# Cross-attention in a perceiver block: the low parts of 64 context channels by another route, and three scalings on ScalarE

## The reference, cut to what matters

```python
xn = layernorm(ctx, ln_x_g, ln_x_b)               # 8 x 1601 x 192
ln = layernorm(latents, ln_l_g, ln_l_b)           # 8 x 64 x 256
q  = ln @ Wq.T
kv = concat([xn @ Wkv.T, ln @ Wlkv.T], axis=1)    # 1665 keys and values
k, v = kv[..., :256], kv[..., 256:]               # 4 heads of 64
attn = (rmsnorm(q, qn_g) * 64**-0.5) @ rmsnorm(k, kn_g).T      # masked
out  = softmax(attn) @ v                          # then Wo, bias, residual
```

## Time and profile before

| what | value |
|---|---|
| runs | 520.67 us median of 3 (520.42 to 523.8) |
| the profiled execution | 520.81 us, its span 519.0 us |
| granted TensorE clock, mean | 0.964 |
| busy: PE, DVE, ACT, POOL | 83%, 78%, 46%, 48% |
| loop over the 56 groups | from 51.8 us (first `key_sums`) to some 325 us |
| mixer and experts | from some 357 us to the end |

### The profile page before, as it was taken

How to read it: one execution, slowest core, us unless ns; L and a number is a source line. 1 busy time by engine, 2 the same in 40 slices (tenths; PEclk the granted TensorE clock), 3 DMA queues, 4 the chain that set the end, 5 groups by cost and what they waited for, 6 DMA issues and landing times.

```text
span 519.0 us, 6624 instructions
## 1 busy us (share of the span) xinstructions
PE 431.1 (83%) x2042; PEld 334.5 (64%) x2042; DVE 405.3 (78%) x969; ACT 237.8 (46%) x547; POOL 250.3 (48%) x264
## 2 busy tenths in 40 slices
PE   3786557779799889887998988887997877899996
PEld 0364335567677677675786867774474765678885
DVE  5847799999999999999988896625659556887776
ACT  0238645267466564664654744331233125335551
POOL 5451956658558557576484553001431232445550
PEclk9999988889999999999899999899999988889999
DMA  8605842022141041222200000920000000000001
GB/s 248 179 1 148 237 135 56 2 90 53 51 141 50 3 141 50 76 67 58 90 3 1 1 1 15 406 97 0 0 2 0 1 0 0 1 1 1 0 2 41
DMA packets 23976, 31.80 MB, mean 61 GB/s; under 512 B 2955, under 2 KB 19653, under 8 KB 23941
## 3 DMA queue, kind: packets, MB, share of 16 engines
q1 hardware_dynamic: 23940, 31.38, 19.6%
HBM read 30.69 MB, written 0.52 MB: 60 GB/s over the span
## 4 chain that ended last, share of the span: by engine, by line
DVE 34%; PE 30%; POOL 21%; issue 8%; ACT 4%; DMA 2%; SPq 1%; DVEq 0%; POOLq 0%; ACTq 0%
PE bank L573 29%; POOL kr L483 12%; DVE kss L1397 5%; DVE arena L1409 4%; DVE arena L1445 3%; DVE split_b L1388 3%; POOL crs L448 3%; DVE cst L1334 2%; DVE arena L1604 2%; DVE arena L1618 1%; DVE kguard L1400 1%; POOL split_b L472 1%; DVE big L1319 1%; POOL cguard L449 1%; DMA mask_in<-in_p_mask 1%
## 5 line engine op out<-in xcount | busy, mean ns | idle before, releaser
L573 PE MATMUL bank<-keyq,split_b 128*128 128x512 f32 (+2 forms) x724 | 171.0, 384 | 21.2 <-DVE split_b L1678 6.7
L573 PEld LDWEIGHTS bank<-keyq,split_b 128*128 128x128 f32 (+1 forms) x724 | 124.7, 194 | 51.3 <-issue 18.0
L483 POOL TENSOR_TENSOR kr<-kguard,neg_half 128x8 f32<-128x8 f32 (+1 forms) x56 | 94.4, 1686 | 103.5 <-DVE kguard L1400 103.1
L573 PE MATMUL bank<-arena 128*128 128x193 f32 (+4 forms) x528 | 103.4, 340 | 18.5 <-ACT arena L1133 9.0
L573 PEld LDWEIGHTS bank<-arena 128*128 128x128 f32 (+2 forms) x528 | 86.9, 195 | 31.1 <-issue 13.9
L1126 ACT ACTIVATE arena<-bank 128x512 f32<-128x512 f32 (+1 forms) x56 | 31.5, 563 | 59.9 <-PE bank L573 59.4
L573 PE MATMUL bank<-split_b,keyq 128*128 128x512 f32 x204 | 51.7, 405 | 0.1
L1409 DVE TENSOR_TENSOR arena<-bank,kr 128x512 f32<-128x512 f32 (+1 forms) x56 | 36.1, 645 | 19.3 <-POOL kr L483 19.1
L1388 DVE TENSOR_TENSOR split_b<-arena,split_b 32x256 fp32r<-32x256 f32 (+1 forms) x112 | 48.0, 428 | 2.5
L573 PEld LDWEIGHTS bank<-split_b,keyq 128*128 128x128 f32 x204 | 39.1, 197 | 8.0 <-DVE split_b L1669 0.2
L472 POOL TENSOR_TENSOR split_b<-arena,split_b 128x256 fp32r<-128x256 f32 (+1 forms) x56 | 38.2, 682 | 10.1 <-ACT split_b L1109 10.0
(11 more groups left out here) (222 smaller groups left out, 620.5 us busy)
## 6 DMA issues: line engine op xcount, KB each, us to landing
arena<-in_ctx SPq DMA_DIRECT2D x16, 576.0 KB, 4.4
arena<-in_p_ctxT SPq DMA_DIRECT2D x8, 800.5 KB, 6.7
arena<-in_p_ctxT SPq DMA_DIRECT2D x8, 400.2 KB, 7.1
arena<-in_p_experts SPq DMA_DIRECT2D x1, 2688.0 KB, 18.4
arena<-in_p_experts SPq DMA_DIRECT2D x1, 2304.0 KB, 12.2
arena<-in_p_experts SPq DMA_DIRECT2D x1, 1536.0 KB, 6.4
X<-in_x SPq DMA_DIRECT2D x1, 512.0 KB, 3.7
arena<-in_t_Wlkv SPq DMA_DIRECT2D x1, 512.0 KB, 7.0
```

Source lines behind the costliest of these rows:

```text
L483: pool.tensor_tensor(kr[0:r, n % 2, 0:k], kg_[0:r, n % 2, 0:k], neg_half[0:r, 0:4 * k].rearrange("p (t h) -> p t h", h=H), ALU.pow).then_i ...
L573: return nc.tensor.matmul(out_, l, r, start=start, stop=stop, skip_group_check=shared)
```

## The change

1. `split_side` goes from VectorE. POOL subtracts instead, right after `split_rest(n)`: one operation of 64 partitions x 256 into a new tile `side_low` (two buffers). ScalarE then issues two SBUF-to-SBUF DMAs per group, each of 32 partitions x 1 KB, that bring it to partitions 96 to 127 (`move_side`). TensorE's `keys(n)` waits for the transfers.
2. ScalarE's split becomes two functions with a semaphore each. In step g = 5, `split_small(u+2)`, with the wait for `spread_sd`, moves behind `square_keys(u)`.
3. `evac_sum`: VectorE keeps the reduction and the reciprocal, ScalarE scales and copies, two operations of 128 x 193. `evac_latent_out` goes to ScalarE, two of 128 x 128. `max_diagonal`: VectorE keeps the reduction, ScalarE makes the diagonals, two of 128 x 128.
4. `cguard` goes: line 1400 takes the larger of `cve` times 64e-16 and the plain sum of squares, both 64 times what they were, so that the power -0.5 now holds the factor 64**-0.5 too; `qkg` loses that factor, and the copy of the latents' scores gets it.

```diff
@@ gpsimd
-                then(pool.tensor_scalar(cguard[:, k, of], cve[:, k, of], 1e-16, None, ALU.mult))
...
                 pool.tensor_tensor(v[:, 1, 0:k], raw[:, 0], v[:, 0, 0:k].bitcast(F32), ALU.subtract).then_inc(xs_rest, 1)
+                pool.wait_ge(xs_small, n + 1)
+                if n >= 2:
+                    pool.wait_ge(side_in[(n - 2) % 3], 32 * ((n - 2) // 3 + 1))
+                pool.tensor_tensor(side_low[:, n % 2, 0:k], raw[0:SMALL, 1], v[0:SMALL, 2, 0:k].bitcast(F32), ALU.subtract).then_inc(xs_side, 1)
@@ tensor, keys(n)
-                pe.wait_ge(xs_side, n + 1)
+                pe.wait_ge(side_in[n % 3], 32 * (n // 3 + 1))
@@ scalar
                 if g == 0:
                     act.wait_ge(ctxT_in[b % 2], 48 * (b // 2 + 1))
-                    act.wait_ge(sd_in[b % 2], 32 * (b // 2 + 1))
...
-                A(xs[n % 3][:, 0, 0:k], ctxT[b % 2][:, 0, 256 * g:256 * g + k], ACT.Copy)
-                A(xs[n % 3][0:96, 2:4, 0:k], ctxT[b % 2][0:96, 1:2, 256 * g:256 * g + k].broadcast_to([96, 2, k]), ACT.Copy).then_inc(xs_split, 1)
+                A(xs[n % 3][:, 0, 0:k], ctxT[b % 2][:, 0, 256 * g:256 * g + k], ACT.Copy).then_inc(xs_split, 1)
+
+            def split_small(n):
...
+                if g == 0:
+                    act.wait_ge(sd_in[b % 2], 32 * (b // 2 + 1))
+                k = 256 if g < NG - 1 else TAIL
+                A(xs[n % 3][0:96, 2:4, 0:k], ctxT[b % 2][0:96, 1:2, 256 * g:256 * g + k].broadcast_to([96, 2, k]), ACT.Copy).then_inc(xs_small, 1)
+
+            def move_side(n):
...
+                act.wait_ge(xs_side, n + 1)
+                for j in range(2):
+                    act.dma_start(xs[n % 3][96:P, 2 + j, 0:k].bitcast(F32), side_low[32 * j:32 * j + 32, n % 2, 0:k].bitcast(F32)).then_inc(side_in[n % 3], 16)
...
+            def max_diagonal(b):
+                act.wait_ge(col_max, b + 1)
+                for pair in range(NPAIR):
+                    last = A(diag[:, pair, :], ident[:], ACT.Copy, scale=qmax[:, pair:pair + 1])
...
+            def evac_sum(b):
+                act.wait_ge(rl_ready, b + 1)
...
+                for pair in range(NPAIR):
+                    last = A(ysb[:, pair, :], y_bank[:, pair * D:pair * D + ROW], ACT.Copy, scale=rl[:, pair:pair + 1])
...
+            def evac_latent_out(b):
+                act.wait_ge(olat_mm, b + 1)
...
+                    last = A(olat[:, pair, :], misc[:, pair * P:(pair + 1) * P], ACT.Copy, scale=rl[:, pair:pair + 1])
...
@@ scalar, the loop
-            split_high(0)
-            split_high(1)
+            for n in range(2):
+                split_high(n)
+                split_small(n)
+            for n in range(2):
+                move_side(n)
...
                 if u + 2 < groups:
                     split_high(u + 2)
+                    if g != 5:
+                        split_small(u + 2)
...
                 if u < groups:
                     square_keys(u)
+                if g == 5 and u + 2 < groups:
+                    split_small(u + 2)
+                if u + 2 < groups:
+                    move_side(u + 2)
...
+                if g == 1 and 1 <= b <= B:
+                    max_diagonal(b - 1)
...
+                if g == 3 and 2 <= b <= B + 1:
+                    evac_sum(b - 2)
+                    evac_latent_out(b - 2)
@@ vector
-                for j in range(2):
-                    last = V.tensor_tensor(v[96:P, 2 + j, 0:k], side_[32 * j:32 * j + 32], v[32 * j:32 * j + 32, 2 + j, 0:k].bitcast(F32), ALU.subtract)
-                last.then_inc(xs_side, 1)
...
-                V.scalar_tensor_tensor(kg_[0:r, n % 2, 0:k], kss[0:r, n % 2, 0:k], 1.0 / DH,
-                                       cguard[0:r, b % 2, 2 * g:2 * g + k].unsqueeze(2).broadcast_to([r, k, H]), ALU.mult, ALU.max).then_inc(k_ss, 1)
+                V.scalar_tensor_tensor(kg_[0:r, n % 2, 0:k], cve[0:r, b % 2, 2 * g:2 * g + k].unsqueeze(2).broadcast_to([r, k, H]), DH * 1e-16,
+                                       kss[0:r, n % 2, 0:k], ALU.mult, ALU.max).then_inc(k_ss, 1)
...
-                then(V.reciprocal(rl[:], lsum[:]))
                 if b:
-                    dve.wait_ge(yT_mm, b)
-                V.tensor_tensor(ysb[:], y[:, :, 0:ROW], rl[:].unsqueeze(2).broadcast_to([P, NPAIR, ROW]), ALU.mult).then_inc(y_evac, 1)
...
+                    dve.wait_ge(olat_evac, b)
+                V.reciprocal(rl[:], lsum[:]).then_inc(rl_ready, 1)
```

More of the change, by code:

```diff
@@ L177, in build @@
         csd = sb("csd", [P, FULL + 1])
-        cguard = sb("cguard", [P, 2, FULL + 1])
         sdT = sb("sdT", [FULL + 1, P])
+        side_low = sb("side_low", [SMALL, 2, 256], F32R)
         sd_part = sb("sd_part", [FULL + 1, 2, P], F32R)
@@ L1136, in exponentials @@
                     A(lat_tile(b), lat_tile(b), ACT.Exp).then_inc(exp_done, 1)
+            def max_diagonal(b):
+                act.wait_ge(col_max, b + 1)
+                for pair in range(NPAIR):
+                    last = A(diag[:, pair, :], ident[:], ACT.Copy, scale=qmax[:, pair:pair + 1])
+                last.then_inc(max_diag, 1)
+            def evac_sum(b):
+                act.wait_ge(rl_ready, b + 1)
+                if b:
+                    act.wait_ge(yT_mm, b)
+                for pair in range(NPAIR):
+                    last = A(ysb[:, pair, :], y_bank[:, pair * D:pair * D + ROW], ACT.Copy, scale=rl[:, pair:pair + 1])
+                last.then_inc(y_evac, 1)
+            def evac_latent_out(b):
+                act.wait_ge(olat_mm, b + 1)
+                if b:
+                    act.wait_ge(o_mm, b)
+                for pair in range(NPAIR):
+                    last = A(olat[:, pair, :], misc[:, pair * P:(pair + 1) * P], ACT.Copy, scale=rl[:, pair:pair + 1])
+                last.then_inc(olat_evac, 1)
             def evac_max(b):
@@ L1435, in max_diagonal @@
                 dve.wait_ge(maxT_mm, b + 1)
-                then(V.tensor_reduce(qmax[:], misc[:, 0:D].rearrange("p (j k) -> p j k", j=NPAIR), AX.X, ALU.max))
-                V.tensor_tensor(diag[:], ident[:].unsqueeze(1).broadcast_to([P, NPAIR, P]), qmax[:].unsqueeze(2).broadcast_to([P, NPAIR, P]), ALU.mult).then_inc(max_diag, 1)
+                V.tensor_reduce(qmax[:], misc[:, 0:D].rearrange("p (j k) -> p j k", j=NPAIR), AX.X, ALU.max).then_inc(col_max, 1)
             def shift_scores(m):
@@ L1526, in _ @@
                 fold_low_part(j)
-            split_side(0)
-            split_side(1)
             for n in range(NG, LEAD):
@@ L1543, in _ @@
                     evac_sum(b - 2)
-                if g == 4 and 2 <= b <= B + 1:
-                    evac_latent_out(b - 2)
                 if g == 1 and 1 <= b <= B:
@@ L1549, in _ @@
                     shift_scores(u - SHIFT)
-                if u + 2 < groups:
-                    split_side(u + 2)
                 if u + LEAD < groups:
```

22 lines of the change are left out of this document (7 added, 15 removed).

## The result

The changed kernel takes 543.71 us (median of 4, 542.5 to 545.71) against 522.0 before (median of 4): ratio 1.042, 95% interval 1.037 to 1.047. It is slower by 4%, and outside the range of the prediction (506 to 534). The profiled execution has a span of 542.1 us against 519.0, at a mean clock of 0.937 against 0.964.

The account below looks back on a forecast made before the run. It took a closed ring of 4.80 us per step as the bound. Four middle batches -1.4, batches 0, 1 and 6 +2.7, batch 7 cancelling, start +0.2, drain +0.8: +2.3 on 520.8 gives 523.1 us, range 506 to 534.

Parts of the forecast that it names:

- The ring: Loop step: reduction, power, `norm_scores`, maximum and shift form a closed ring of 4.80 us; VectorE's other work is mostly cover.
- Parts 1, 2 and 4: Per step: VectorE late at g=3 (-1.26 us) and g=6 (about -0.9); power -0.23; maximum meeting `side_low` +0.49.
- Part 4: GpSimd's `side_low` starts about 0.1 us before VectorE's maximum and holds it: +0.49 us, in the ring.
- Part 3: On GpSimd, `side_low` takes 0.72 us (bounds 0.4 and 0.75), hidden in most steps but not at g = 0 to 2.
- Part 5: ScalarE's added work per batch: 21.07 + 2.0 + 6.4 = 29.5 us of 35, so it fits.
- Part 5, the issue: Each DMA issue on ScalarE takes 0.46 us, 6.4 us per batch.
- rival B: Slower: ScalarE is the bound, 0.83 us per issue, 11.6 per batch, with 1.5 of waits on top; 533 us, chance 0.23.
- Part 5, the transfer: Transfer takes 2.5 us from issue to landing, issued some 7 us before `keys(n)`'s result is due: costs nothing.
- Start +0.2: Start: two issues and two waits before `fold_high_part`, but VectorE no longer splits there: +0.2 us.
- Drain +0.8: Drain: twice the sum becomes two ScalarE operations, and the diagonal is a hop more: +0.8 us.

Follow-up runs that it names:

- w1_no_low_part: The kernel before without `split_side`, the low part of the last 64 channels left as zeros; 505.69 us, ratio 0.9695.
- w2_sync_spread: The changed kernel with SyncE waiting for `side_low` and issuing its transfers, and the mixer loads issued one a step; 528.17 us, ratio 1.010.
- w2_later_issue: The changed kernel with ScalarE's wait and two issues moved half a step later, behind `scale_context(u)`; 534.33 us.
- w1_scalings: The changed kernel without the side route: scalings on ScalarE, no `cguard`, `split_side` on VectorE again; 527.26 us, ratio 1.0105.
- w3_loads_apart: w2_sync_spread with the last two batches' scalings and last diagonal on VectorE, and large loads cut apart behind each step's side transfers; 532.61 us.
- w4_loads_due: w3_loads_apart with context's first load back at g = 0 and the turned context at g = 1 and 2; 518.91 us, ratio 0.994.

## Why the prediction was wrong

It forecast 523.1 us and got 543.7. By its own steps:

- **What bounds the kernel: right.** The ring of `key_sums`, power, `norm_scores`, maximum and shift. w1_no_low_part shows it, and the 50.0 us of waits for the power.
- **Parts 1, 2 and 4: right but for one step, and to be seen only where nothing blocks ScalarE.** In batch 3 of w2_sync_spread the step g = 5 takes 5.04 us (foretold 5.06), g = 3 4.75 after 6.01 (-1.26, foretold -1.0), g = 6 4.51 after 5.05 (-0.54, foretold -0.45), g = 0 to 2 together 15.30 after 14.87 (+0.43, foretold +0.35). Only g = 4 was foretold 0.5 too long: 4.56, unchanged. The batch is 1.1 us shorter than before (34.15 after 35.29), where the forecast had 0.35. VectorE and GpSimd of that batch at g = 3 to 5 (w2_sync_spread):

```profile
174.60 0.69 DVE L1474 TENSOR_TENSOR arena<-arena 128x512 f32<-128x512 f32 x1
...
179.17 1.16 DVE L1474 TENSOR_TENSOR arena<-arena 128x512 f32<-128x512 f32 x1
```

```profile
175.62 0.87 POOL L491 TENSOR_TENSOR side_low<-arena,split_b 64x256 fp32r<-64x256 f32 x1 [1.09 <-ACT split_b L1134]
176.77 1.64 POOL L502 TENSOR_TENSOR kr<-kguard,neg_half 128x8 f32<-128x8 f32 x1 [0.28 <-DVE kguard L1450]
...
179.06 0.72 POOL L491 TENSOR_TENSOR side_low<-arena,split_b 64x256 fp32r<-64x256 f32 x1
```

  `side_low` starts at 179.06, the maximum at 179.17, and it takes 1.16 instead of 0.69: the meeting of the earlier trace rows, as Part 4 had it. At g = 4 `side_low` waited for the small split and started (175.62) after the maximum had ended. The power takes 1.64. The step's price, 0.47, was right to 0.02.
- **Part 3: right.** `side_low` takes 0.72 us on 64 partitions.
- **Part 5: wrong, and this is the step that failed.** It said that the wait at the head of `move_side` "stands behind `square_keys(u)`, and behind it are only splits for two steps on". Behind it stands the whole of ScalarE's next step: splits, deviations, exponentials, square, the diagonal and the copy of the maximum. GpSimd's `side_low` stands behind its own scales at g = 0 to 2, ScalarE waits for it, and the exponentials and the square reach TensorE and VectorE late. Moving the wait half a step gave 9.4 us back (8.8 of them in batches 1 to 7, by the profiles; for these the forecast had 0.4 in all, and the changed kernel lost 10.0), giving wait and issues to SyncE with loads spread 15.5 (543.7 to 528.2). The part summed busy time (29.5 of 35 us: "it fits"); it fitted, and was late.
- **Part 5, the issue: mis-sized, with little effect in the loop.** 0.58 us each (1.16 a pair), between the forecast's 0.46 and rival B's 0.83. Rival B came nearest in time (533), by luck more than by its mechanism: its first term, ScalarE full of issues, did not come (23 us busy and 8 of issues in 36), and of its second, the waits on top, it had only 1.5 us a batch.
- **Part 5, the transfer: "nothing" was wrong.** Its median, 1.9 us from issue to landing, is hidden in most steps. But pairs that ScalarE issued while loads of context were in flight took up to 6.9 us, and at the end of batch 0 that was longer than the cover: `keys` waited 8.05 us and the step is 3.5 longer than before. In SyncE's queue, behind such loads, it was late in several steps.
- **Start +0.2: mis-sized.** The first `key_sums` is 1.2 us late, and batch 0 adds 5.8, in a step of 7.85 (before 5.57), whose `keys` ran at the lower clock behind a gap of 3.52 us in TensorE (4.12 us instead of 2.5; its pair of transfers had landed only 0.1 us before it started), and in the one of 7.83, by the late transfer. Both stayed when the wait was moved (w2_later_issue).
- **Drain +0.8: mis-sized.** 6.1 us. The hand-overs to ScalarE (the sum twice and the diagonal once) cost 3.3 to 3.9 of it: from the last `key_sums` to the end w2_later_issue takes 201.0 us at 0.96, the clock of before in the first 45.5 us, and w1_scalings 201.6 at 0.92, where five kernels with the scalings on VectorE at 0.96 take 197.3 to 197.8. The rest goes with the lower clock (0.81): the last projection's four matmuls took 2.08 us instead of 1.13.

What is not settled: what decides where TensorE's clock falls. Every kernel of this study has some such spells; in the drains of the changed kernel, w3_loads_apart and w4_loads_due it fell behind a gap of TensorE, and before's drain has a gap of the same kind without one.

## What to carry to other kernels

A wait costs the engine that holds it and everything behind it in that engine's program, however idle the engine is: before putting a wait on another engine's late result, list the next step's instructions of the waiting engine and who needs them, and put the wait where its event is already past, or on a queue on which nothing urgent stands. Price a small transfer by what large loads are in flight when it is issued, in its own queue or another, and not by its median. Taking work from a busy engine pays only where that engine is in the ring; here 49 us of work were worth 17. A load moved later must still meet the due time of whoever reads furthest ahead.
